# A long convolution moved into the block of a top-32 weighting: kernel transform beside the first search, values folded with the film weights

## What is computed

```python
scores = einsum('bthd,bghd->bhtg', Q, K) / sqrt(DH)
topv, topi = top_k(scores, 32)
attn = zeros_like(scores).at[..., topi].set(softmax(topv))
V = x_vision @ Wv
c_t = einsum('btg,bgd->btd', attn.mean(axis=1), V) * text_mask[..., None]
x = layernorm(x_text, g_norm_in, b_norm_in)
scale_in, shift_in = split(c_t @ W_film_in + b_film_in, 2)
x = x * (1.0 + mod_gate * scale_in) + mod_gate * shift_in
y = s4d(x, ...)                       # irfft(rfft(x) * rfft(K)) + x * D_skip
scale_out, shift_out = split(c_t @ W_film_out + b_film_out, 2)
y = y * (1.0 + mod_gate * scale_out) + mod_gate * shift_out
xt = x_text + y
h = gelu(layernorm(xt, g_ffn, b_ffn) @ W1 + b1) @ W2 + b2
return layernorm(xt + h, g_norm_out, b_norm_out)
```

## Time and profile before

| | us |
|---|---|
| three runs: lowest, median, highest | 1701.76, 1704.51, 1705.24 |
| the profiled execution | 1701.49 |
| its span in the trace | 1699.7 |
| PE busy in the span | 1396.9 (82%) |
| DVE busy | 1276.4 (75%) |
| ACT busy | 896.2 (53%) |
| POOL busy | 643.9 (38%) |

### The profile page before, as it was taken

How to read it: one execution, slowest core, us unless ns; L and a number is a source line. 1 busy time by engine, 2 the same in 40 slices (tenths; PEclk the granted TensorE clock), 3 DMA queues, 4 the chain that set the end, 5 groups by cost and what they waited for, 6 DMA issues and landing times. The chain is left out here.

```text
span 1699.7 us, 19910 instructions
## 1 busy us (share of the span) xinstructions
PE 1396.9 (82%) x6780; PEld 741.5 (44%) x6781; DVE 1276.4 (75%) x2873; ACT 896.2 (53%) x1409; POOL 643.9 (38%) x412
## 2 busy tenths in 40 slices
PE   5777799999997667988889898887857539999798
PEld 2222344333343522555555555555645323333465
DVE  4999577855516679999999999998947566676433
ACT  4665211566623303777778777778811236666321
POOL 2665212022102001878788787878800030000012
PEclk9899899999997978999999999999977758999999
DMA  6000111000008520000000000000020120000000
GB/s 149 1 1 0 34 56 42 0 1 0 0 0 189 105 63 1 1 1 1 1 1 1 1 1 1 1 1 1 1 99 2 37 66 1 1 1 1 1 1 13
DMA packets 30967, 37.33 MB, mean 22 GB/s; under 512 B 13983, under 2 KB 24990, under 8 KB 29730
## 3 DMA queue, kind: packets, MB, share of 16 engines
q1 hardware_dynamic: 28302, 23.91, 5.1%
q10 hardware_dynamic: 2552, 12.02, 3.4%
HBM read 29.68 MB, written 6.24 MB: 21 GB/s over the span
## 5 line engine op out<-in xcount | busy, mean ns | idle before, releaser
L1567 PE MATMUL psum<-film_ka,film_context_qa 97*128 97x427 bf16 (+3 forms) x896 | 335.1, 374 | 83.9 <-DVE search_and_weigh_e L1805 42.9
L1569 PE MATMUL psum<-film_kb,film_context_qb 128*128 128x427 bf16 (+3 forms) x896 | 331.4, 371 | 0.0
L1772 DVE MAX8 search_and_weigh_kept<-psum 128x8 f32<-128x213 f32 (+1 forms) x960 | 318.9, 376 | 9.3 <-PE psum L1569 8.7
L1965 ACT ACTIVATE search_and_weigh_e<-psum,search_and_weigh_bias 128x512 f32<-128x512 f32 (+1 forms) x416 | 269.8, 667 | 106.3 <-PE psum L1569 102.6
L1805 DVE SCALAR_TENSOR_TENSOR search_and_weigh_e<-psum,film_context_top,search_and_weigh_e 128x512 f32<-128x512 f32 (+1 forms) x325 | 231.9, 720 | 10.8 <-ACT search_and_weigh_e L1965 8.1
L1838 POOL TENSOR_TENSOR search_and_weigh_e<-search_and_weigh_e 128x1024 f32<-128x1024 f32 (+1 forms) x91 | 206.9, 2273 | 7.1
L1567 PEld LDWEIGHTS psum<-film_ka,film_context_qa 97*128 97x128 bf16 x896 | 93.1, 104 | 205.9 <-DVE search_and_weigh_kept L1772 86.3
L1828 POOL TENSOR_TENSOR search_and_weigh_e<-search_and_weigh_e,search_and_weigh_keep 128x512 f32<-128x512 f32 (+1 forms) x91 | 102.0, 1121 | 155.4 <-ACT search_and_weigh_keep L1944 153.5
L1866 PEld LDWEIGHTS psum<-ctx_rows,search_and_weigh_mean_T 128*128 128x128 f32 (+1 forms) x816 | 124.8, 196 | 31.3 <-issue 5.3
L3080 POOL TENSOR_TENSOR residual<-residual,top_expert_kept 128x1024 f32<-128x1024 f32 x7 | 16.5, 2354 | 292.4 <-DVE top_expert_kept L3037 292.4
L2843 DVE TENSOR_REDUCE gqa_attend_low<-psum 128x1 f32<-128x128 f32 (+7 forms) x128 | 94.1, 755 | 43.3 <-PE psum L2762 40.8
(11 more groups left out here) (550 smaller groups left out, 2540.2 us busy)
## 6 DMA issues: line engine op xcount, KB each, us to landing
film_kb<-film_k_rows ACTq DMA_DIRECT2D x4, 1601.0 KB
film_ka<-film_k_rows ACTq DMA_DIRECT2D x3, 1601.0 KB
ctx_T<-in_ctx_T SPq DMA_DIRECT2D x1, 2401.5 KB
gqa_experts_w<-in_L_ffn_W SPq DMA_DIRECT2D x1, 2048.0 KB
film_convolve_back<-in_dft_back SPq DMA_DIRECT2D x1, 1728.0 KB, 12.7
film_k_rows<-cross_attention_film_hi SPq DMA_DIRECT2D x6, 256.0 KB, 2.1
film_k_rows<-cross_attention_film_mid SPq DMA_DIRECT2D x6, 256.0 KB, 2.0
film_k_rows<-cross_attention_film_low SPq DMA_DIRECT2D x6, 256.0 KB, 2.0
```

Source lines behind the costliest of these rows:

```text
L1567: pe.matmul(out, a["qa"][0:ROWS, h, rows], a["ka"][0:ROWS, h, c + b:c + b + cols], start=True, stop=False)
L1569: last = pe.matmul(out, a["qb"][:, h, rows], a["kb"][:, h, c + b:c + b + cols], start=False, stop=True)
L1772: last = dve.max(kept[:, h % 2, PER_PIECE * u + s, :], bank[:, lo:hi])
L1965: act.activation(e[:, n % RING, sub, 0:PIECES[u][1]], ps[:, SEARCH_BANKS + q % WEIGH_BANKS, 0:PIECES[u][1]], ACT.Exp, bias=bias[:, i % 2, ...
```

## The change

`film_convolve`, `search_general` and `weigh_again` have no blocks of their own any more. One block, `film_stage`, holds the search and weighing, one branch per engine (`if_flagged`) over both the general search and the second weighing, and the convolution.

* `split_queries` also multiplies Wv with both film weight matrices (one PE matmul of 128x512), stores the product `w_vf` to DRAM, and takes the statistics of `xn` for the second norm (8 + 8 small DVE instructions, a root on ACT behind its fetches).
* At the block's begin POOL transforms the kernel (`transform_on_pool`), ACT normalises `xn` into the room of `c_T`, POOL applies gain and shift; PE runs the nine forward slots between search pieces 20 to 44 (`KERNEL_AT`, `kernel_slot`), ACT copies them to `kf` inside the `e` ring, and SP stores `u` and `kf` to DRAM. ACT's first exponential waits for both stores.
* The flags, their count and its read move from the end into the last tile's weighing (`COUNT`, `READ_COUNT`).
* The context tiles are transposed one by one as they are finished; the film of the inner scale and shift is one product of the context with `w_vf` (8 matmuls of 128x256) in place of two products one after the other; the same for the outer one.
* After the last scores SP fetches `u`, the tables, `kf` and the rest into the room of the keys (`ka`, `kb`). DVE then works in halves of four tiles; POOL makes the outer film's rows and adds.
* The `recycle` that stood between `weigh_again` and `film_convolve` stands between `film_stage` and `film_out_ffn`; the number of calls is the same.

```diff
+    with ExitStack() as ctx:
+        split_queries(nc, g, t, Memory(nc, ctx, "split_queries"), a)
+    a.update(film_places(a))
+    with ExitStack() as ctx:
+        film_stage(nc, g, t, Memory(nc, ctx, "film_stage"), a)
+    recycle(nc, Memory.used)
+    with ExitStack() as ctx:
+        film_out_ffn(nc, g, t, Memory(nc, ctx, "film_out_ffn"), a)
```

```diff
+            sp.wait_ge(w_vf_ready, 1)
+            sp.dma_start(a["w_vf_store"], w_vf[:]).then_inc(w_vf_stored, 16)
+            sp.wait_ge(w_vf_stored, 16)
...
+            for i in range(NT):
+                last = dve.bn_stats(stats[:, i, :], xn[:, i, :])
...
+            dve.tensor_scalar(again, mv[:, :, 1], LN_EPS, None, ALU.add).then_inc(var_again, 1)
+            dve.wait_ge(root_again, 1)
+            link(dve.reciprocal(again, again))
+            link(dve.scalar_tensor_tensor(out=minus_mean, in0=mv[:, :, 0], scalar=-1.0, in1=again, op0=ALU.mult,
+                                          op1=ALU.mult))
...
+            pe.wait_ge(film_loaded, 16 * 3)
+            pe.matmul(ps[0:DC, 4, :], w_v_T[:], w_film[:], start=True, stop=True).then_inc(w_vf_done, 1)
...
+            act.wait_ge(w_vf_done, 1)
+            act.activation(w_vf[:], ps[0:DC, 4, :], ACT.Copy).then_inc(w_vf_ready, 1)
...
+            act.wait_ge(var_again, 1)
+            act.activation(again, again, ACT.Sqrt).then_inc(root_again, 1)
```

```diff
+                if searching and NH * G + sub == LAST_PICK:
+                    dve.wait_ge(picked, PICKS * NH * NT)
+                    dve.tensor_tensor(a["flags"][:], eighth[:], a["top"][:, :, TOP - 1], ALU.is_gt).then_inc(flagged, 1)
+                if searching and NH * G + sub == READ_COUNT:
+                    in_all = total[0:1, 0:1]
+                    dve.wait_ge(counted, 1)
+                    dve.tensor_copy(a["count"][:, 0:NT * NH], ps[0:1, 0, 0:NT * NH])
+                    link(dve.reduce_sum(in_all, ps[0:1, 0, 0:NT * NH], AX))
+                    dve.tensor_copy(a["count"][:, NT * NH:], in_all).then_inc(f["count_ready"], 1)
...
+                    if searching and r in KERNEL_AT:
+                        kernel_slot(pe, g, f, KERNEL_AT.index(r))
+                if searching and NH * G + sub == COUNT:
+                    pe.wait_ge(flagged, 1)
+                    pe.matmul(ps[0:1, 0, 0:NT * NH], b["column"][:], a["flags"][:], start=True,
+                              stop=True).then_inc(counted, 1)
...
+        pe.wait_ge(f["w_film_loaded"], 16)
...
+            if i == NT - 1:
+                pe.wait_ge(tok_ready, NT)
+                pe.transpose(ps[0:DC, 6, 3 * P:4 * P], c_tok[:], g["ident"][:]).then_inc(cc_psum, 1)
+            pe.wait_ge(cc_ready, i + 1)
+            last = pe.matmul(ps[:, i // 2, (i % 2) * 2 * D:(i % 2 + 1) * 2 * D], c_ctx[:, i * P:(i + 1) * P],
+                             f["w_vf"][0:DC, :], start=True, stop=True)
+            if i % 4 == 3:
+                last.then_inc(film_done, 1)
...
+            if n % NCH == NCH - 1 and n >= NCH:
+                copy_context(n // NCH - 1)
```

```diff
+KF_COPIES = ((0, 2), (2, 5), (5, 7), (7, 9))
+KERNEL_AT = (20, 22, 24, 26, 28, 38, 40, 42, 44)
...
+def kernel_slot(pe, g, f, slot):
+    if slot == 0:
+        pe.wait_ge(f["ahead_early"], 16)
+        pe.wait_ge(f["k_even"], 1)
+    if slot == N_EVEN:
+        pe.wait_ge(f["k_odd"], 1)
+    if slot == 7:
+        pe.wait_ge(f["kf_ready"], 1)
+    n0, n1 = next(x for x in KF_COPIES if x[0] <= slot < x[1])
+    transform_forward(pe, f["early"]["ahead"], f["early"]["v_k"], kernel_banks(g, n0, n1)[:, slot - n0],
+                      slot).then_inc(f["k_psum"], 1)
```

```diff
+            sp.wait_ge(f["u_made"], 1)
+            sp.dma_start(a["u_store"], g["c_T"][:]).then_inc(f["u_stored"], 16)
+            sp.wait_ge(f["kf_ready"], len(KF_COPIES))
+            sp.dma_start(a["kf_store"].rearrange("p (r c d) -> p r c d", c=2, d=D),
+                         early["kf"]).then_inc(f["kf_stored"], 16)
...
+            sp.wait_ge(first["picked"], first["all_picked"])
+            sp.dma_start(f["w_vf"][0:DC, :], a["w_vf_store"][:, 0:2 * D]).then_inc(f["w_film_loaded"], 16)
...
+            sp.wait_ge(first["score_done"], first["all_scores"])
+            with if_flagged(sp):
+                sp.wait_ge(general_over, 1)
+            sp.dma_start(u, a["u_store"].rearrange("p (i d) -> p i d", d=D)).then_inc(u_loaded, 16)
             sp.dma_start(ahead[:, 0:N_EVEN], t["dft_ahead"][:, 0:N_EVEN]).then_inc(ahead_even, 16)
             sp.dma_start(ahead[:, N_EVEN:], t["dft_ahead"][:, N_EVEN:]).then_inc(ahead_odd, 16)
...
+            sp.dma_start(kf, a["kf_store"].rearrange("p (r c d) -> p r c d", c=2, d=D)).then_inc(kf_loaded, 16)
+            sp.dma_start(back[:, 0:N_EVEN], t["dft_back"][:, 0:N_EVEN]).then_inc(back_even, 16)
+            sp.dma_start(back[:, N_EVEN:], t["dft_back"][:, N_EVEN:]).then_inc(back_odd, 16)
+            sp.dma_start(w_vo[0:DC, :], a["w_vf_store"][:, 2 * D:]).then_inc(out_loaded, 16)
+            sp.dma_start(rows_out, t["L1_xattn_b_film_out"].unsqueeze(0).to_broadcast([P, 2 * D])
+                         .rearrange("p (c d) -> p c d", d=D)).then_inc(out_loaded, 16)
```

```diff
+            pe.wait_ge(f["column_set"], 1)
+            first["tensor"](pe)
+            with if_flagged(pe):
+                general["tensor"](pe)
+                again["tensor"](pe)
...
+                transform_back(pe, back, yf, slot_of(z_banks, KF_COPIES, slot), slot).then_inc(z_psum, 1)
+            pe.wait_ge(out_loaded, 32)
+            pe.wait_ge(z_ready, 1)
+            for i in range(NT):
+                last = pe.matmul(flat[:, OUT_BANK * HALF + i * 2 * D:OUT_BANK * HALF + (i + 1) * 2 * D],
+                                 g["c_T"][0:DC, i * P:(i + 1) * P], w_vo[0:DC, :], start=True, stop=True)
+                if i % 4 == 3:
+                    last.then_inc(out_done, 1)
```

```diff
         def _(pool):
-            pool.wait_ge(out_copied, 2)
-            pool.tensor_tensor(a["moved"][:], a["film_out"][:, :, 1, :], g["xn"][:], ALU.add)
+            link = chained(pool, chain_pool)
+            early = f["early"]
+            pool.memset(b["column"][:], 1.0).then_inc(f["column_set"], 1)
+            transform_on_pool(pool, link, g["k_tok"], early["v_k"], early, f["k_even"], f["k_odd"])
+            pool.wait_ge(f["normed"], NT)
+            pool.wait_ge(f["rows_early"], 32)
+            link(pool.tensor_tensor(early["u"], early["u"], tiles(early["gain"]), ALU.mult))
+            pool.tensor_tensor(early["u"], early["u"], tiles(early["shift"][:]), ALU.add).then_inc(f["u_made"], 1)
+            first["pool_sums"](pool)
+            with if_flagged(pool):
+                again["pool_sums"](pool)
+
+            pool.wait_ge(out_loaded, 32)
+            pool.wait_ge(f["gate_loaded"], 16)
+            link(pool.tensor_tensor(rows_out, rows_out, gate.unsqueeze(1).to_broadcast([P, 2, D]), ALU.mult))
+            link(pool.tensor_tensor(moved, g["xn"][:], tiles(rows_out[:, 1, :]), ALU.add))
+            link(pool.tensor_scalar(rows_out[:, 0, :], rows_out[:, 0, :], 1.0, None, ALU.add))
+            for n in range(2):
+                four = slice(4 * n, 4 * n + 4)
+                pool.wait_ge(out_copied, n + 1)
+                pool.tensor_tensor(film_out[:, four, 0, :], film_out[:, four, 0, :], tiles(rows_out[:, 0, :], 4), ALU.add)
+                pool.tensor_tensor(moved[:, four], film_out[:, four, 1, :], moved[:, four], ALU.add)
```

551 lines of the change are left out of this document (291 added, 260 removed).

## The result

The changed kernel takes **1677.03 us** (median of 4 runs, 1674.07 to 1678.04) against 1704.88 for the kernel before beside it (1701.76 to 1706.23): a ratio of 0.9836, 95% interval 0.9817 to 0.9855, 27.9 us between the medians. The forecast was 1676.5 with a range of 1664 to 1688. Its profiled execution took 1676.14, its span is 1674.4.

What follows compares the result with a forecast made beforehand. Bound: DVE through search and weighing, then an 82 us latency chain (1234 to 1316) with one engine working. 32.6 + 1.1 - 1.1 - 5.5 - 1.1 = 26.0 us gained from 1701.5 gives 1675.5, put 1 higher: 1676.5, range 1664 to 1688.

Steps and rivals of the forecast that it cites:

- A: From the last weighing work until the film is applied: u complete at 1245.5 instead of 1278.1, gain 32.6 us.
- the bound on two jumps: Ahead of the convolution: two jumps cost at most 9.5 us, read from DVE's 11.14 us idle; one some 4.
- B: From the film to the inverse's end: 36.1 us instead of 37.2, POOL's disturbance included, gain 1.1 us.
- The exclusion: Convolution: POOL and DVE instructions with two SBUF inputs block each other, adding 1.2 us in u's transform, 5.1 in the inverse.
- C: Begin of the next block: 1.64 us with the recycle in between instead of 0.53, loss 1.1 us.
- D: Inside the search: PE's 32 float32 matmuls for the kernel's transform lose 5.5 us, bounds 0 and 14.
- half of the matmuls at each clock: Search: 16 matmuls at 1.2 GHz, 0.43 us each, and 16 at 2.4, 0.23 each, 10.6 us before slack.
- a first exponential 4 to 7 us later: End of the search: profile sign that the slots' loss is right, ACT's first exponential 4 to 7 us after 665.55.
- E: Small additions: flags, reads and a cast in the last tile 0.8 us, root in `split_queries` 0.3, loss 1.1 us.
- better: Rival: the search absorbs the slots (loss 2 us) and POOL's collisions cost 2 instead of 6, giving 1669; chance 0.20.
- The tail at 1.2 GHz: Rival: PE stays at low clock in the back transform or a jump is late, 1683 to 1686; chance 0.14.
- three times that: Rival: POOL's `tensor_scalar` three times as slow, the transformed kernel not ready in the search, 1687; chance 0.04.

Runs made afterwards that it cites:

- e9: The kernel before the change, unmodified, run and profiled a second time; 1703.74 us, ratio 1.0008.
- e6: Changed kernel with each of the inner film's eight PE matmuls made twice; 1681.21 us, ratio 0.9866 to the kernel before.
- e2: Changed kernel without the general search and second weighing, branches and bodies removed on all five engines; 1677.63 us, ratio 0.9853 to the kernel before.
- e10: Changed kernel with DVE transforming the convolution's kernel once more behind its jump; 1688.06 us, ratio 0.9922 to the kernel before.
- e3: Changed kernel without POOL's seven outer film instructions, the next block adding the rows itself; 1672.72 us, ratio 0.9835 to the kernel before.
- e4: Changed kernel with PE's outer film right behind its jump and POOL's sums waiting for u's even slots; 1676.84 us, ratio 0.9848 to the kernel before.
- e7: Changed kernel with kernel slots beside the picks, outer film ahead of PE's jump and one POOL sum left; 1666.53 us, ratio 0.9782 to the kernel before.
- e1: Changed kernel with PE's nine kernel slots moved to search pieces beside DVE's picks; 1674.39 us, ratio 0.984 to the kernel before.
- e5: The changed kernel, unmodified, run and profiled once more; 1678.76 us, ratio 0.9846 to the kernel before.
- e8: e7 with the inner film of tiles 0 to 5 made during the last tile's weighing; 1669.11 us, ratio 0.9798 to the kernel before.
- e11: e7 with DVE's two bias instructions moved from behind its jump into the last tile; 1667.64 us, ratio 0.9796 to the kernel before.

## Why the prediction was right

**A, gain 32.6 expected, 32.0 measured.** From the last weighing work to u's transform it was 1278.13 - 1232.75 = 45.4 us and is 1251.28 - 1237.92 = 13.4. Against e9's profile of the kernel before it is 42.5 - 13.4 = 29.1, so the agreement within 0.6 us is partly luck: the bound on two jumps was read off one profile, and the next one had 2.9 us less there. The film on PE is the path (e6), the jump is hidden but for 0.3 us (e2). Its size was wrong: "some 4" was put in, and it lasted 5.9 us on DVE and 6.1 on PE; reading the count and jumping cost 0.7 on SP, where 4 had been put in for the jump. The sum gave DVE 5.3 us of room and PE 7.3. So DVE's jump overran its room a little: its rows were ready at 1245.1, and by e2 the film's first half some 0.3 us before. Some 8 of the 32 are the kernel's transform (e10: 9.3 us in this stretch, 1.2 of them the meeting with POOL). The shares of the second norm, of the folded product and of the blocks were not taken apart.

**B, gain 1.1 expected, 2.6 measured.** The exclusion is shown by e3, e4 and e7. Its size: I had both engines' time add up in full in the inverse, 5.1 us; it was 14.1 against 10.0 (1271.70 to 1285.83), 4.2, since DVE gets an instruction in between two of POOL's. In the odd transform it cost DVE 2.7 and the path 0.5 instead of 1.2: from the start of u's transform to the first product it is 10.98 us, without POOL (e3) 10.45. The Trainium skill ("SBUF — State Buffer", Who interferes with whom) speaks of an exclusive lock. By that rule the trace agrees: the DVE instruction that met `moved` in e4 ended at 1252.2, 0.5 us behind POOL's, where it takes 0.69 alone.

**C, loss 1.1 expected, 1.3 measured** (1.83 us of idle ahead of 1287.65).

**D, loss 5.5 expected, 3.4 measured**, and against the first profile of before this was the term furthest off. The mechanism was right (e1). The step that failed is "half of the matmuls at each clock": the first two slots ran at 1.2 GHz and half of the sixth, the others at 2.4 as in the row at 629.88, and PEclk from 611 to 662 rose from 0.80 to 0.86. With 5.5 of the 32 matmuls at the low clock, the prediction's own sum gives 5.5 x 0.43 + 26.5 x 0.23 - 5 = 3.5 us. Its sign, a first exponential 4 to 7 us later, was missed: it came 3.4 later. In e1, with the slots where PE idled, the search was shorter than with no slots at all.

**E, loss 1.1 expected, 1.7 measured**, by tiles: eighth tile 74.0 against 72.95, last 54.6 against 53.9. The flags instruction took 0.98 us in the eighth. It takes 0.97 in e7 as well, whose eighth tile lost only 0.2 us; there the granted clock was 1.00 from 1114 to 1122 us, where it was 0.79 at that place in the tile both before and in the changed kernel. So the loss of the eighth tile goes with that clock too, and what the flags alone cost is not shown. In the last, PEclk was 0.60 where it had been 0.80 for 8 us; e7 has the same count in the same place and 53.8, so those 0.7 are not the count's. Whether the 0.3 us for the root of `split_queries` were lost is not shown: the search began at 611.49 and before at 611.42, but over the thirteen profiles it begins anywhere from 608.2 to 614.7.

**The sum**: 32.0 + 2.6 - 1.3 - 3.4 - 1.7 = 28.3 us against 26.0. The median landed 0.5 us above the forecast, and the profiled execution 0.6 above the sum's 1675.5, because the rest of that execution was 2.9 us longer, which I had at nothing. That part of the agreement is chance: e9's profile of before and e10's differ by as much in the same code. Against e9's profile the three stretches give 25.3 us, and the medians of e5 and of the kernel before beside it are 25.4 apart, so 26.0 lies inside what was measured, and no closer agreement than some 3 us can be claimed.

Of the rivals, "better" was half true, with the two terms it named, by 2.1 and 1.5 us instead of 3.5 and 4. "The tail at 1.2 GHz" was not seen: the back transform ran at 0.39 us a pair. POOL's `tensor_scalar` took 0.85 us for 128x256 where its sum took 0.72, not three times that, and the transformed kernel was complete at 649.1. PE's granted clock over the weighing was 0.98, as before.

## What to carry to other kernels

Work that is moved beside a loop goes where the bound engine has its long steps: the same nine slots cost 3.4 us between DVE's short pieces and nothing beside its picks. A POOL instruction beside DVE work with two SBUF inputs costs DVE most of its length (4.2 us for four sums of 5.1), so give it a start condition that puts it beside PSUM reads; otherwise a transfer decides where it falls. Work that is put ahead of a jump can run during it: the same eight matmuls waited 6.3 us behind PE's jump in e4 and covered 3.4 us of it in e7. And before a difference of a few us between two profiles is explained, cut both at the same instructions and profile one kernel twice: here unchanged code took 4.9 us more in a second profile of one kernel, and 7.7 lay between the ends of the column.

## What was not expected of the hardware

* A taken jump over a long body lasted, from the branch to the engine's next instruction, 5.9 us on DVE in the changed kernel and 4.6 in e4, 5.3 on ACT in e7, and 5.5 and 6.0 on POOL (changed kernel, e4). PE's record of its branch lasted 6.1, 6.4 and 6.2 (changed kernel, e4, e7). SP needed 0.7 with its load of the count; its body is one wait. The same jump of the same kernel need not repeat: 3.6 and 0.5 us over `search_general` in the two profiles of before, which stays open. The Trainium skill ("Runtime: NRT & Kernel Launch", Instruction fetch mechanics) has a taken branch wait for a fetch where its target is outside the fetched window; the short body's 0.7 agrees with that.
* With more work on PE its granted clock was higher: 0.91 to 0.92 over the search with slots among the picks (e1, e7, e8, e11), 0.81 with none in both profiles of before, and the search was 0.3 to 0.6 us shorter.
* Tile lengths of the weighing repeat within 0.1 us over the seven profiles that share the first slot table; e7 and e11 agree with each other as well, while e1, with their table, has 2.8 us more (570.22 against 567.42). In all thirteen profiles 310.0 to 316.3 us pass from the attention to the end in code that is the same. The mean granted clock there was 0.95 in the shortest and 0.93 in the longest; what sets it stays open.
